# Inputs of one stage turned two slots earlier, five loads fewer per pass, and the last block product made in two halves

## What is computed

```python
x = _layernorm(x + _L0_gnn_ref(x, adj, ...))   # Chebyshev, two products with adj
x = _layernorm(x + _L1_gnn_ref(x, 0, ...))     # two times adj, weights, relu
x = _layernorm(x + _L2_gnn_ref(x, adj, ...))   # x @ w_self + (adj @ x) @ w_neighbor + bias
x = _layernorm(x + _L3_gnn_ref(x, adj, ...))   # x, adj x, adj adj x, one weight matrix for all
```

## Time and profile before

| what | us |
|---|---|
| median of 3 runs | 1239.7 (1238.35 to 1241.29) |
| the profiled execution | 1236.85 |
| its span, first to last instruction | 1235.0 |
| outside the span | 1.85 |
| TensorE busy, of the span | 1174.2 (95%) |
| VectorE, ScalarE, GpSimd busy | 859.8, 498.3, 344.5 |
| mean granted TensorE clock | 0.988 |

### The profile page before, as it was taken

The page is one execution under the profiler, slowest core; times in us unless marked ns, Lnnn a source line. Parts: engine busy times, 40 slices in busy tenths (PEclk is TensorE's granted clock), DMA queues, the critical chain, the costliest instruction groups (busy, mean ns, idle before and its releaser), DMA issues.

```text
span 1235.0 us, 16680 instructions
## 1 busy us (share of the span) xinstructions
PE 1174.2 (95%) x5539; PEld 968.0 (78%) x5539; DVE 859.8 (70%) x1864; ACT 498.3 (40%) x666; POOL 344.5 (28%) x208
## 2 busy tenths in 40 slices
PE   8999999999999999899999999998989999979894
PEld 6888888888888787777878887887778888868783
DVE  5836888786778877998246286877678774725856
ACT  6621111121111101111176666675646756544652
POOL 0001121021024533753022032335436341411312
PEclk9999999999999999999999999999999999989998
DMA  9732121331124221321633545437554266796553
GB/s 362 320 102 61 39 68 49 80 100 43 46 63 128 62 67 31 94 69 41 213 153 154 166 158 159 165 121 216 159 152 112 70 156 143 177 257 192 184 169 133
DMA packets 183326, 161.59 MB, mean 131 GB/s; under 512 B 121728, under 2 KB 141728, under 8 KB 181952
## 3 DMA queue, kind: packets, MB, share of 16 engines
q1 hardware_dynamic: 170272, 113.24, 31.0%
q10 hardware_dynamic: 12960, 47.19, 11.6%
HBM read 115.83 MB, written 44.56 MB: 130 GB/s over the span
## 4 chain that ended last, share of the span: by engine, by line
PE 70%; DMA 10%; DVE 10%; SPq 6%; issue 3%; ACT 1%; POOL 0%; DVEq 0%; ACTq 0%; POOLq 0%
PE ps L1607 19%; PE ps L1189 13%; PE ps L1191 12%; PE ps L1494 8%; PE ps L1495 8%; PE ps L1512 6%; DMA B<-tf 4%; SPq L1424 4%; DVE nat L1897 2%; DVE ring L1897 2%; PE ps L1542 2%; PE ps L1543 2%; DMA ring_g<-td 2%; DMA raw<-in_at 1%; DMA td<-raw 1%
## 5 line engine op out<-in xcount | busy, mean ns | idle before, releaser
L1189 PE MATMUL ps<-B,ops 128*128 128x512 f32 x1008 | 403.9, 401 | 18.0 <-DMA B<-tf 16.0
L1191 PE MATMUL ps<-B,ops 128*128 128x512 f32 x1008 | 395.6, 392 | 0.0
L1607 PE MATMUL ps<-Tw,xs 128*128 128x512 f32 x1280 | 309.8, 392 | 7.5 <-DVE ring L1897 7.2
L1239 ACT CAST B<-pk 128x1024 fp32r<-128x1024 fp8e4 x245 | 248.8, 1045 | 151.0 <-PE ps L1191 146.8
L1607 PEld LDWEIGHTS ps<-Tw,xs 128*128 128x128 f32 x1280 | 238.2, 188 | 64.8 <-DVE ring L1897 9.6
L1189 PEld LDWEIGHTS ps<-B,ops 128*128 128x128 f32 x1008 | 191.2, 190 | 63.4 <-DMA B<-tf 22.3
L1191 PEld LDWEIGHTS ps<-B,ops 128*128 128x128 f32 x1008 | 191.2, 190 | 37.1
L1494 PE MATMUL ps<-B,xs 128*128 128x512 f32 x512 | 200.3, 391 | 1.9 <-DVE xs L1798 1.9
L1495 PE MATMUL ps<-B,xs 128*128 128x512 f32 x512 | 199.3, 389 | 0.0
L1897 DVE SCALAR_TENSOR_TENSOR nat<-ps,embn,nat 128x128 f32<-128x128 f32 x448 | 153.6, 343 | 41.3 <-PE ps L1607 40.5
L1897 DVE SCALAR_TENSOR_TENSOR ring<-ps,embn,ring 128x128 f32<-128x128 f32 x512 | 175.4, 342 | 0.0
(11 more groups left out here) (116 smaller groups left out, 1269.2 us busy)
## 6 DMA issues: line engine op xcount, KB each, us to landing
B<-tf ACTq DMA_DIRECT2D x90, 512.0 KB, 4.0
raw<-in_at SPq DMA_DIRECT2D x10, 1024.0 KB, 15.4
td<-raw SPq DMA_DIRECT2D x31, 256.0 KB, 2.7
tf<-B SPq DMA_DIRECT2D x15, 512.0 KB, 2.6
raw<-in_at SPq DMA_DIRECT2D x12, 512.0 KB, 8.8
zd<-nat SPq DMA_DIRECT2D x24, 256.0 KB, 2.9
stg<-zd SPq DMA_DIRECT2D x24, 256.0 KB, 6.0
tb<-stq SPq DMA_DIRECT2D x40, 128.0 KB, 2.1
```

Source lines behind the costliest of these rows:

```text
L1189: pe.matmul(bank, ops[:, slot, 0, m, :], of, start=not more and m == 0, stop=False, skip_group_check=more)
L1191: mm = pe.matmul(bank, ops[:, slot, 1, m, :], of, start=False, stop=m == 7, skip_group_check=more)
L1239: eng.copy(to, of).then_inc(s_exA, 1)
L1607: mm = pe.matmul(ps[:, 4 + 2 * p + q, :], src, Tw[:, wi, 512 * p:512 * p + 512], start=i == 0, stop=i == 4)
```

## The change

Three edits, all in the nine passes:

1. `AHEAD` puts `flip` and `flipped` of stage 4 at w - 7, and `flipback` and `biased` at w - 6. Stage 5 keeps 5 and 4. The planner of the buffers (`turn_plan`) gets the longer times; it needs three turn buffers as before.
2. In stage 4 the piece `m` = 5 of each block product is cast by ACT, where it was loaded: 10 loads a pass are left of 15, in two passes. In the last block product of the last pass all pieces are cast by ACT, so its three loads go too.
3. That last block product is made in two halves: all eight units of node half `q` = 0 first, then those of `q` = 1, each unit with 2 matmuls and a piece of 128 by 512 (16 casts of half size). `whole` of `q` = 0 then waits for the first half alone, and the last two chunks are weighed at slots 27 and 29 where they were at 29 and 30.

```diff
-EXPANDS = {2: "AAVAAVAV", 3: "AADAADAD", 4: "AADAADAD", 5: "AAAAAAAV", 6: "AADAADAD"}
+EXPANDS = {2: "AAVAAVAV", 3: "AADAADAD", 4: "AADAAAAD", 5: "AAAAAAAV", 6: "AADAADAD"}
...
+def halved(n, i):
+
+    return n == len(PASSES) - 1 and i == 6
+
+def ended(n, i, q):
+
+    return SLOTS * n + 4 * (i + 1) - (2 if halved(n, i) and q == 0 else 0)
...
-            out += [(SLOTS * n + 4 * i + m // 2, Unit(n, i, 2, m)) for m in range(8)]
+            if halved(n, i):
+                out += [(SLOTS * n + 4 * i + 2 * q + m // 4, Unit(n, i, q, m)) for q in range(2) for m in range(8)]
+            else:
+                out += [(SLOTS * n + 4 * i + m // 2, Unit(n, i, 2, m)) for m in range(8)]
...
+AHEAD = {4: 7, 5: 5}
+
-LAST_WEIGH = [17, 18, 21, 22, 25, 26, 29, 30]
+LAST_WEIGH = [17, 18, 21, 22, 25, 26, 27, 29]
...
-    return EXPANDS[PASSES[e // 40][1]][e % 8]
+    return EXPANDS[PASSES[e // 40][1]][e % 8] if e < 40 * len(PASSES) - 8 else "A"
...
             for x, (i, _, _) in enumerate(SUMS):
-                put(t0 + 4 * (i + 1), 1, "whole", n, x, q)
+                put(ended(n, i, q), 1, "whole", n, x, q)
...
-                put(w - 5, 5, "flip", j, p, c)
-                put(w - 5, 8, "flipped", j, p, c)
-                put(w - 4, 9, "flipback", j, p, c)
-                put(w - 4, 4, "biased", j, p, c)
+                put(w - AHEAD[p], 5, "flip", j, p, c)
+                put(w - AHEAD[p], 8, "flipped", j, p, c)
+                put(w - AHEAD[p] + 1, 9, "flipback", j, p, c)
+                put(w - AHEAD[p] + 1, 4, "biased", j, p, c)
...
-                        for q in range(2):
+                        for q in [h] if h < 2 else [0, 1]:
...
+                    if s.c < 2:
+                        to, of = to[:, 512 * s.c:512 * s.c + 512], of[:, 512 * s.c:512 * s.c + 512]
```

More of the change, by code:

```diff
@@ L508, in y_plan @@
         at = {w: [SLOTS * n + 4 * (i + 1)] * 2 for i, w in KEPT.items()}
-        at[3] = [SLOTS * (n + 1)] * 2
+        at[3] = [ended(n, 6, q) for q in range(2)]
         for x, (_, _, _, end) in enumerate(chunks(n)):
@@ L518, in turn_plan @@
             for j, _, c, w in chunks(n):
-                yield w - 5, w + 1, ("flip", j, p, c)
+                yield w - AHEAD[p], w + 1, ("flip", j, p, c)
                 if p == 5:
@@ L1077, in unit_end @@
                 def unit_end(n, i, q):
-                    return unit_at[Step("product", n, i, 2, 7)]
+                    return unit_at[Step("product", n, i, q if halved(n, i) else 2, 7)]
                 def operand_slot(n, x):
@@ L1161, in pe_step @@
                         u = Unit(s.j, s.p, s.c, s.k)
-                        n, i, _, m = u
+                        n, i, h, m = u
                         if m == 0:
```

## The result

The changed kernel takes 1224.39 us (median of four runs, 1219.06 to 1227.26), the kernel before beside it 1240.49 (four runs, 1238.35 to 1242.13): a ratio of 0.9866, 95% interval 0.9828 to 0.9905. Faster was right; the size was not. I had forecast 9.9 us and a range down to 1227; the medians lie 16.1 apart. That is the better figure, and still outside my range.

The account below looks back on a forecast made before the run. TensorE, busy 95% of the span, was taken as the bound, with its waits and what follows its last matmul. 7.0 + 1.14 + 1.8 = 9.9 us off the median of 1239.7 gave 1229.8, range 1227 to 1236.

Parts of the forecast that it names:

- Part 1: Stage 4: inputs turned at w - 7 remove all four TensorE waits for turned inputs, 7.0 us; bounds 3.5 to 7.0.
- SP's chain: Stage 4's turned inputs: SP, busy 7.3 of a 7.24 us period, could be full and leave waits; costed at nothing.
- the 0.66 that flips put on VectorE: Stage 4: each flip delays VectorE's sums or `plus` by 0.66 us; costed at nothing, 10.6 without the lead.
- Part 2: Stage 4: casting piece 5 removes its wait, 1.14 us; piece 7's three waits, 2.0, stay; bounds -1.1 to 3.1.
- their end 0.07: Chance left for a time below 1227 us, with the 2.0 us of piece 7's waits in stage 4 gone too.
- the rival of the collision: Earlier flips put transfers where other loads fly, so pieces land late: 4.6 us of gain lost, 1234.4; chance 0.20.
- The size of a wait: TensorE's waits for transfers in stage 4, each priced at its bracket: 7.0 for turned inputs, 3.1 for pieces.
- Part 3: Last block product in halves: VectorE starts 1.27 us earlier, GpSimd's end saves 0.55, together 1.8; bounds -1.2 to 2.5.
- ACT did not bound the end: Rival, last block product: half casts take the full 1.05 us, losing 1.2 where 1.8 was gained, 1232.8; chance 0.08.
- no GpSimd operation held up a sum on TensorE's path: Rival, stage 4: GpSimd delays VectorE's 16 multiplications by 1.46 us each, 23.4 lost, 1253; chance 0.03.

Follow-up runs that it names:

- e1_ahead: The kernel before with only stage 4's earlier flips (w - 7), all 15 loads a pass kept, last block product whole: 1225.09 us, ratio 0.9926.
- e3: The kernel before with only the last block product in halves, all its pieces cast, last chunks weighed at slots 27 and 29: 1234.70 us, ratio 0.9993.
- e11: The kernel before with only the residual's transfers in stages 3 and 6 moved to slots 10, 12, 14 and 15: 1221.74 us, ratio 0.9882.
- e2_pieces: The kernel before with only piece 5 cast in stage 4, 10 loads a pass for 15: 1226.48 us, ratio 0.9931; repeated 1228.65 us, 0.9925.
- e5_seven: The kernel before with only piece 7 cast in stage 4, piece 5 still loaded, 10 loads a pass: 1228.88 us, ratio 0.9946.
- e12_two: The kernel before with only piece 2 cast in stage 4, pieces 5 and 7 still loaded, 10 loads a pass: 1232.68 us, ratio 0.9973.

## Why the prediction was wrong in size

**Part 1** (7.0): right. No `weigh` of stage 4 waits for a transfer, in the changed kernel and in e1_ahead; the lead of w - 7 is enough, SP's chain is not full, and the 0.66 that flips put on VectorE shows in no wait of TensorE.

**Part 2** (1.14, with 2.0 kept): the step that failed. The wait for piece 5 went. I kept the three for piece 7 at 2.0, between bounds of a loss and 3.1, and gave their end 0.07. They went as well. With stage 4 unchanged the waits for piece 7 are 2.0, 1.4 and 2.8 (before, e3, e11), with early flips alone 1.1, with fewer loads alone 2.4 and 2.0, and with both zero in three traces, 0.3 and 1.2 in two. My part 2 named that these loads could land sooner, as the load of piece 5 no longer flies beside them, and took it at nothing. I priced the meeting of the two queues only where a transfer was moved *into* another's way (the rival of the collision); that each edit also moves transfers *out of* the other's way I did not price. The same coupling made e2_pieces worth 8.5 to 9.3 where my step gives 1.14.

**The size of a wait**: the second step that failed. I priced each wait at its bracket. The eight waits of stage 4 were 10.1 in brackets and cost 142.9 - 130.9 = 12.0: 1.9 more, in line with 0.23 to 0.26 for each. The first matmul behind a wait takes 0.50, where it takes 0.39 in an unbroken row, and TensorE's busy time in the stretch fell from 132.09 to 130.0 to 130.7.

**Part 3** (1.8): right: 1.6 between the means, 2.0 between the two traces.

**Sum.** 7.0 + 1.14 + 2.0 + 1.9 + 1.6 to 2.0 = 13.6 to 14.0, and 14.1 (11.1 to 16.9) measured. These sizes are read from the traces afterwards; that they add up is no second forecast. The 16.1 of the first medians hold some 2 us that I count as spread: the traces differ by 2.7 ahead of the change.

**Rivals.** None came true. The loads did not collide more (4.3 became 3.6, and 4.0 with early flips alone), ACT did not bound the end, and no GpSimd operation held up a sum on TensorE's path: TensorE waits for no transfer and no sum in the stretch.

**The range** was too narrow: the sum came out too small, and so did the spread, as four runs of one kernel lay 8 us apart (1219.06 to 1227.26), where I had taken 2.9 from three runs of before.

## What to carry to other kernels

Waits for transfers on different queues are not separate terms: list what is in flight beside each late transfer, and count an edit for every transfer that it takes out of the way, not only for the wait that it is aimed at. Price a wait above its bracket, and higher still where the clock falls behind it. And put bulk transfers that nobody is waiting for where no short-lead load is in flight: moving four of the eight in a pass by a few slots, in four passes, was worth as much as the whole change.

## What I had not expected of the hardware

Short waits can cost TensorE its clock, and not by their length alone. In the trace of before it stood at 0.50 from 753.8 to 757.0, behind a wait of 1.80, and at 1.00 behind the wait of 3.48 (timeline of PE, then the stretch behind each):

```profile
753.15 0.50 PE L1189 MATMUL ps<-B,ops 128*128 128x512 f32 x1 [1.80 <-DMA B<-tf]
```

```profile
753.80:757.00 3.20, 3.20 (x9) 2.52 (x8) 0.56 (x1) 2.14 (x4) 0.90 (x1) 0.50 0.36 147
...
919.50:926.00 6.50, 6.50 (x37) 5.70 (x38) 3.71 (x8) 3.00 (x4) 1.41 (x2) 1.00 0.52 115
```

What decides it these runs do not settle. In stage 4 it fell behind waits of 2.10, 2.35 and 2.59 (e5_seven, e3_halves, e12_two) and not behind one of 2.60 (e11_refill_alone). It may be part of why executions of one kernel lie several us apart: e3_halves and the kernel before have the same stage 4, and only e3_halves lost clock there.

How long a load of 512 KB takes depends on what flies beside it. Over the 14 traces, the 398 loads that met nothing or only other loads of pieces took 3.27 in the median; the 159 that met a store of a turned input for 1 us or more took 4.35, up to 5.81; beside four transfers of 256 KB the one above took 8.14.
